# Attention and a routed expert layer on one core: one-hots shared 17, 9 and 6, the seatless test moved up, rank products and idle products around the last tile's rows

## What is computed

```python
x = x + xattn(layernorm(x), ctx, ctx)      # 8 heads of 8 rows, softmax over 256 columns
h = layernorm(x)
logits = h @ gate                          # 8 experts
w, idx = top_k(logits, 2); w = softmax(w)
for each token, for its two experts e:
    out += w[e] * (silu(h @ w0[e]) * (h @ w1[e])) @ wo[e]
x = x + out
```

## Time and profile before

| | |
|---|---|
| median of 3 runs | 489.21 us (484.64 to 489.81) |
| the profiled execution's own time | 489.81 us |
| its span (first to last instruction) | 488.1 us |
| mean granted TensorE clock | 0.931 |
| TensorE matmul busy | 426.1 us, 87% |
| VectorE busy | 303.1 us, 62% |
| ScalarE busy | 267.1 us, 55% |
| GpSimd busy | 219.9 us, 45% |

### The profile page before, as it was taken

How to read it: one execution, slowest core, us unless ns; L and a number is a source line. 1 busy time by engine, 2 the same in 40 slices (tenths; PEclk the granted TensorE clock), 3 DMA queues, 4 the chain that set the end, 5 groups by cost and what they waited for, 6 DMA issues and landing times.

```text
span 488.1 us, 10784 instructions
## 1 busy us (share of the span) xinstructions
PE 426.1 (87%) x3468; PEld 212.4 (44%) x3469; DVE 303.1 (62%) x636; ACT 267.1 (55%) x529; POOL 219.9 (45%) x244
## 2 busy tenths in 40 slices
PE   4857999889899999998666799999999999999991
PEld 4322343324343444333232455555555555566650
DVE  7799898898888888976867734343434343222220
ACT  2555898778778788977414444444444444222220
POOL 9544322181809052339628233454545454536231
PEclk9775899989889999999867999999999999999997
DMA  8757569685859682426994112333333333323322
GB/s 246 215 165 201 153 165 215 205 245 173 247 165 245 178 255 75 151 71 234 395 389 150 36 34 45 42 57 43 54 47 50 49 50 53 55 45 46 41 22 23
DMA packets 42246, 65.03 MB, mean 133 GB/s; under 512 B 6297, under 2 KB 32218, under 8 KB 42202
## 3 DMA queue, kind: packets, MB, share of 16 engines
q1 hardware_dynamic: 28570, 38.49, 28.0%
q0 software_dynamic: 11328, 23.86, 20.9%
q10 hardware_dynamic: 2304, 2.10, 1.4%
HBM read 39.53 MB, written 24.58 MB: 131 GB/s over the span
## 4 chain that ended last, share of the span: by engine, by line
PE 67%; DVE 10%; ACT 7%; DMA 6%; POOL 4%; issue 2%; ACTq 1%; SPq 1%; DVEq 0%; POOLq 0%
PE max_ps L1658 19%; PE pv_ps L1525 9%; PE pv_ps L1680 6%; PE ring_ps L1508 6%; ACT pt L851 5%; PE max_ps L1652 4%; PE max_ps L1384 4%; PE ring_ps L1680 4%; DVE mx L1026 4%; PE ring_ps L1616 3%; PE ring_ps L1405 2%; PE ring_ps L1675 2%; DMA Q<-mrow 2%; DMA Q<-q_img 2%; PE ring_ps L1416 2%
## 5 line engine op out<-in xcount | busy, mean ns | idle before, releaser
L1026 DVE TENSOR_REDUCE mx<-max_ps 128x4 f32<-128x1024 f32 x128 | 150.7, 1218 | 20.7 <-PE max_ps L1384 20.6
L851 ACT ACTIVATE pt<-ring_ps 128x512 f32<-128x512 f32 x256 | 139.2, 599 | 32.6 <-PE ring_ps L1508 29.1
L1658 PE MATMUL max_ps<-w_sb,pt 128*128 x224 | 101.6, 596 | 1.0 <-issue 1.0
L778 POOL DMA_INDIRECT out<-rb,sidx x34 | 54.8, 1613 | 81.3 <-DVE rb L1358 37.0
L1525 PE MATMUL pv_ps<-pt,w_sb 128*27 128x256 f32 (+2 forms) x1024 | 82.7, 408 | 0.7 <-ACT pvs L861 0.4
L1330 DVE TENSOR_TENSOR pt<-pt,max_ps 128x512 f32<-128x512 f32 x34 | 23.4, 688 | 68.4 <-issue 49.2
L1384 PE MATMUL max_ps<-K,Q 48*128 48x256 bf16 x512 | 54.5, 294 | 12.2 <-DVE mx L1026 12.0
L1508 PE MATMUL ring_ps<-Q,K 50*128 50x256 f16 x512 | 53.4, 289 | 11.5 <-ACT pt L851 9.2
L1658 PEld LDWEIGHTS max_ps<-w_sb,pt 128*128 128x128 f32 x224 | 40.3, 190 | 42.2 <-issue 42.0
L935 ACT ACTIVATE pt<-ring_ps 128x512 f32<-128x512 f32 x34 | 20.3, 598 | 68.1 <-PE ring_ps L1616 68.1
L1508 PEld LDWEIGHTS ring_ps<-Q,K 50*128 50x128 bf16 x512 | 15.1, 96 | 65.3 <-ACT pt L851 58.2
(11 more groups left out here) (230 smaller groups left out, 650.6 us busy)
## 6 DMA issues: line engine op xcount, KB each, us to landing
w_sb<-in_L_ffn_w_kernel POOLq DMA_DIRECT2D x16, 512.0 KB, 12.4
K<-k_img SPq DMA_DIRECT2D x14, 448.0 KB, 6.2
Q<-q_img SPq DMA_DIRECT2D x14, 448.0 KB, 7.6
k_img<-kpart SPq DMA_DIRECT2D x28, 192.0 KB, 3.8
q_img<-qpart SPq DMA_DIRECT2D x28, 192.0 KB, 3.4
wo_sb<-in_L_ffn_wo_kernel POOLq DMA_DIRECT2D x8, 512.0 KB, 14.4
acc<-pvs SPq DMA_DIRECT2D x6, 512.0 KB, 3.1
wo_sb<-in_ctx ACTq DMA_DIRECT2D x16, 128.0 KB, 3.9
```

The source lines that it names most:

```text
L778: g.indirect_dma_start(xacc, bass.IndirectOffsetOnAxis(ap=sidx[sl.par][:, 0:1], axis=0), y_sb[sl.par], None, compute_op=ALU.add).then_inc( ...
L851: a.activation(pt[:, (2 * i + h) % PTN, :, :], bank(key)[:, :, :], ACT.Exp, scale=SCALE).then_inc(ring_read, 1)
L1026: v.tensor_reduce(mx[:, t % 2, :, :, p].rearrange("q mt h -> q h mt"), max_ps[n % 2][:, :, :, :], axis=AX.X, op=ALU.max).then_inc(max_read, 1)
L1658: last = nc.tensor.matmul(flat(max_ps[sl.par][:, bank_of]), lhsT=xT[sl.par][:, k * P:(k + 1) * P], rhs=weight(w, e, KC, k), start=(k == 0) ...
```

## The change

It has four parts. In the last tile, the reordering of tile 14 moves from head 2 to head 1, the transposes and logits of units 5 and 6 move one head later, rank product 0 moves to head 6 and rank product 1 behind the last reordering and the logits of tile 14, followed by two new idle products into the bank of `pv_ps`; VectorE's rank sums move to match. The one-hots are shared 17 (VectorE), 9 (ScalarE) and 6 (GpSimd), where it was 16, 8 and 8. The first half of the seatless test moves in front of the first gathered rows on TensorE and in front of the weight products on VectorE, and its second half moves from slot 1 to slot 0.

```diff
-    rows_at[T - 1, 1] = ST - 3
-    logits_at[T - 1, 2] = ST - 3
-    rows_at[T - 1, 3] = ST - 2
-    logits_at[T - 1, 4] = ST - 2
-    unperm_at = {(T - 2, 1): 0, (T - 2, 4): 1, (T - 1, 2): 2}
+    rows_at[T - 1, 2] = ST - 3
+    logits_at[T - 1, 3] = ST - 3
+    rows_at[T - 1, 4] = ST - 2
+    logits_at[T - 1, 5] = ST - 2
+    unperm_at = {(T - 2, 1): 0, (T - 2, 4): 1, (T - 1, 1): 2}
...
-    ranks_at = {(T - 1, 2): 0, (T - 1, 7): 1}
+    ranks_at = {(T - 1, 6): 0}
...
-        by_act = [(k, t) for k in range(TOPK) for t in range(2, T, 4)]
-        by_pool = [(k, t) for k in range(TOPK) for t in range(3, T, 4)]
+        by_act = [(0, t) for t in (3, 7, 11, 14)] + [(1, t) for t in (2, 5, 8, 11, 14)]
+        by_pool = [(0, t) for t in (5, 10, 15)] + [(1, t) for t in (4, 9, 13)]
+        by_dve = [(k, t) for k in range(TOPK) for t in range(T) if (k, t) not in by_act + by_pool]
...
             norm_last(normed_last[0:2], x2_last[0:2], 0, 1)
-            ranks(0)
...
             norm_last(normed_last[2:3], x2_last[2:3], 2, 2)
-            ranks(1)
+            ranks(0)
...
             norm_last(normed_last[3:4], x2_last[3:4], 3, 3)
+            ranks(1)
             choose(ST, unit_tiles[ST])
...
             then(v.tensor_tensor(pay[:, 1], wts[:, :, :], pay[:, 0], ALU.subtract))
+            v.wait_ge(spare_turned, 1)
+            then(v.tensor_reduce(spare_any[:, :], y_ps[1][0:NT, 0, P // 2:P].bitcast(f16), axis=AX.X, op=ALU.max))
+            v.tensor_tensor(spare_diag[:, :], identh[0:NT, 0:NT], spare_any[:, 0:1].broadcast_to([NT, NT]),
+                            ALU.mult).then_inc(diag_done, 1)
             v.wait_ge(rows_picked, TOPK)
...
                 if sl.peeled and sl.t == 0:
-                    turned_spares()
+                    spread_back()
...
-            def keep_warm(n):
+            def keep_warm(n, to=max_ps[1][:, 1]):
 
                 for _ in range(n):
-                    nc.tensor.matmul(flat(max_ps[1][:, 1]), lhsT=ident[:, :], rhs=flat(xn), start=True, stop=True)
+                    nc.tensor.matmul(flat(to), lhsT=ident[:, :], rhs=flat(xn), start=True, stop=True)
...
             for m in range(ST - 1, UNITS):
                 turn_rows(m)
                 logits(m)
+                if m < UNITS - 1:
+                    rank(1)
+                    keep_warm(2, pv_ps)
...
             pe.wait_ge(slots_done, 1)
+            turn_spares()
             turn_x(Slots(0, 0))
...
                 if sl.peeled and sl.t == 0:
-                    turn_spares()
+                    spread_spares()
                 if sl.peeled and sl.t == 1:
-                    spread_spares()
                     slot_weights()
```

More of the change, by code:

```diff
@@ L1232, in _ @@
                                 iota_t[:, None, :].broadcast_to([P, T, NTL]), ALU.is_equal).then_inc(rows_picked, 1)
-                onehots(k, [t for t in range(T) if (k, t) not in by_act and (k, t) not in by_pool])
+                onehots(k, [t for n, t in by_dve if n == k])
             v.wait_ge(told_full, 1)
@@ L1302, in stage, with spread_back @@
                     v.tensor_copy(wo_st[n][:, 0:FC // 2, :], wo_sb[:, bass.ds(e * FC, FC // 2), :]).then_inc(wo_copied[0], 1)
-            def turned_spares():
-                v.wait_ge(spare_turned, 1)
-                then(v.tensor_reduce(spare_any[:, :], y_ps[1][0:NT, 0, P // 2:P].bitcast(f16), axis=AX.X, op=ALU.max))
-                v.tensor_tensor(spare_diag[:, :], identh[0:NT, 0:NT], spare_any[:, 0:1].broadcast_to([NT, NT]),
-                                ALU.mult).then_inc(diag_done, 1)
-                then(v.tensor_scalar(rtok[:, :], tok[:, :], 1.0, None, ALU.max))
-                then(v.reciprocal(rtok[:, :], rtok[:, :]))
-            def slot_rows():
+            def spread_back():
                 v.wait_ge(spare_full, 1)
@@ L1316, in slot_rows @@
                 v.wait_ge(spare_read, 1)
+                then(v.tensor_scalar(rtok[:, :], tok[:, :], 1.0, None, ALU.max))
+                then(v.reciprocal(rtok[:, :], rtok[:, :]))
+            def slot_rows():
                 then(v.tensor_tensor(spare_of[:, :], spare_of[:, :], spare_own[:, :], ALU.add))
@@ L1584, in _ @@
                     else:
-                        pe.wait_ge(told_done, k * T // 2 + t // 4 * 2 + t % 4 + 1)
+                        pe.wait_ge(told_done, by_dve.index((k, t)) + 1)
                     last = nc.tensor.matmul(pv_ps[:, 0, 0:NTL], lhsT=onehot_s[:, k, t, :], rhs=onehot_t[:, k, t, :],
```

## The result

The changed kernel takes 484.31 us in the median of 20 runs (478.84 to 489.14), the kernel before 488.60 in the median of 20 beside them (482.71 to 493.13). The ratio is 0.9927, 95% interval 0.9898 to 0.9956: 0.7% faster. That is 3.6 us by the ratio (as by the means of all 20) and 4.3 by the medians, where I forecast 4.2. Executions of either kernel scatter by 2.6 to 2.7 us (standard deviation), so whole times can't tell parts of 1 us; the rows can.

The account below looks back on a forecast made before the run. TensorE bounds the expert stage; before it a chain across engines, where only shortening the last-ending piece saves time. Terms 1.0 + 0.6 + 1.4 - 0.1 + 1.3 = 4.2 us off the 489.21 median give 485.0 us, range 482.8 to 488.8.

Parts of the forecast that it names:

- F: Stretch from GpSimd's first weight load to its first one-hot, forecast to shorten by 1.6 us.
- the slot weights: Slot 1: TensorE's 1.28 us wait for VectorE's reading of the spread spares goes; 1.3 us saved, bounds 0.9 and 1.4.
- The last tile's heads: TensorE, last tile: two waits removed, one added; last reordering starts 1.0 us sooner, bounds -0.5 and 1.8.
- Rival C: Clock falls to half in head 1 at the added wait, until the tile's end; 4.6 us slower, 493.8, chance 0.05.
- One of my signs of being wrong: Last tile: the last reordering starts no sooner after head 0 than before.
- VectorE's moved sums hidden: Last tile: moved rank sums fit VectorE's waits, 1 us to spare for the first, about 0.7 for the second; no loss.
- Idle products: Before the last rows: they keep TensorE's clock up for gate products and transposes; 0.6 us saved, bounds -0.9 and 0.7.
- full clock from 243 on: Sign of being right, last tile: TensorE's clock stays full from 243 on, with gate products at 0.58 us.
- One-hots: GpSimd's one-hots cut from eight to six, so the sum product ends earlier; 1.4 us saved, bounds 0.9 and 1.6.
- VectorE's 17 would not hold GpSimd up: One-hots: GpSimd runs beside VectorE and ends at 261.7; the rival that it is held up had chance 0.06.
- The seatless test: Its transposition moves before the first gathered transposes on TensorE; costs 0.1 us, bound -0.3; VectorE's added work hidden.
- The idle products behind the sum: After the one-hots' sum: six records take 4.5 to 5.4 us, up to 0.5 us late at half clock.

Follow-up runs that it names:

- e8: Kernel before with only the seatless test moved up; median 488.20 us against 489.22 beside it, ratio 0.9890.
- e3: Changed kernel without the two idle products behind the moved rank product; median 485.35 us, ratio to the kernel before 1.0025.
- e4: Changed kernel with two idle products instead of three behind the one-hots' sum; median 485.66 us, ratio to the kernel before 0.9965.
- e7: Kernel before with only the one-hots shared 17, 9 and 6; median 487.30 us against 489.22 beside it, ratio 0.9969.
- e6: Kernel before with only the part around the last tile; median 487.40 us against 489.22 beside it, ratio 0.9995.
- e11: Changed kernel, copy before head 1's exponentials, two and a half idle products behind the one-hots, half one behind the first transposes; 482.07 us, ratio 0.9913.
- e12: e11 plus an idle product behind the last slot's hidden layer and half a one behind its transposes; 481.93 us, ratio to the kernel before 0.9851.
- e2: Changed kernel with tile 14's reordering put back at head 2; median 483.36 us, ratio to the kernel before 0.9937.
- e1: Changed kernel with the whole part around the last tile undone; median 485.64 us, ratio to the kernel before 0.9992.

## Why the prediction was right, and where it was not

The time came out at 484.31 against 485.0, the gain at 3.6 (interval 2.1 to 5.0) or 4.3 by the medians, against 4.2. The mechanism was right in the back half and for the order of the heads at full clock; that the total came so near is in part luck. F gave half of its 1.6 us on average, the slot weights gave more than forecast, and the 489.21 from which I took the gain was 0.6 above the median of twenty. Point by point:

1. The last tile's heads, 1.0 us, set between 1.3 at full clock and 0.45 at half. At full clock the heads came as I had counted them (the last reordering 15.84 us after the first weight load, forecast 15.87), and against the old order that is 1.04, not 1.3. The step that failed is the clock. I let it act on the last two heads, and it fell in heads 1 and 2, behind the wait that the change adds; U was then 0.3 longer than before, in three of five traces. Rival C had this mechanism with the right place; it overpriced it, because the clock was back within 4 us each time. One of my signs of being wrong came true: from head 0's scores to the last reordering the changed kernel took 17.83 us, the kernel before 17.56. What I missed beside it: 0.64 us of wait at the rank product was not the wait's size but what the low clock left of it (1.39 in e8).
2. VectorE's moved sums hidden: right, 0.97 and 0.73 us to spare (forecast 1 and 0.7).
3. Idle products, 0.6 us: right. The gate products gained 0.41 in every trace. From the last reordering to the last choice, traces with an equally long last normalisation differ by 0.59 between the orders (8.09 and 7.50 us with 0.41, 8.37 and 7.78 with 0.69) and by 0.66 between e3 and the others. The idle products ended at 243.3, and the transposes of the last rows began at 244.75. The sign "full clock from 243 on" held up to 248.5 only; then it was half for 3.4 us, where before it was half from 242.9 to 253.1. One thing not foreseen: the last normalisation took 0.69 us instead of 0.41, and from the last reordering to the last choice the changed kernel needs 7.78 us where e4 needs 7.50; 0.3 us of F went there.
4. One-hots, 1.4 us: 1.45, in every trace that has them. That VectorE's 17 would not hold GpSimd up was read rightly from the trace (6.58 us for six, forecast 6.6). The Trainium skill, "SBUF — State Buffer", Who interferes with whom, says that tensor_scalar can enter two-port modes, in which one of the two engines blocks the other fully. No such block came here: GpSimd's one-hots took 0.84 to 0.97 us beside VectorE's and 0.79 with VectorE idle. Whether VectorE's ran in such a mode no trace shows.
5. The seatless test, -0.1: 0.06 to 0.2 (e4). The idle products behind the sum, "up to 0.5 us late": up to 0.85 (e8: X 6.88 against 6.03), because six records took 5.47 us at half clock throughout. My own numbers gave 0.8 and not 0.5 (262.0 + 5.4 = 267.4 against 266.6). It was outside my sum, and it should have been in it: in six of the seven traces that have the moved test and three idle products, X is 0.2 to 0.85 above 6.03 (mean of the seven 6.44, against 5.90 in the three traces without the moved test).
6. Slot weights, 1.3 us: 1.56 at the first output product. I had counted TensorE's idle of 1.28 and not the 0.3 us of the spreading product, which moved in front of slot 0's `turn_inter`, where TensorE waits anyway (0.47 us before, 0.51 after).

By stretches: F gives 0.75 us (mean of old order 33.12, of new with idle products 32.37; four traces each), S 1.45, O 1.54, and X takes 0.3 (the changed kernel's own 6.20 and 6.22) to 0.5: 3.2 to 3.4 us, inside what the whole time shows. That S and O come from the one-hots and the seatless test is shown by the runs that have one part alone (e7, e8) and by e6, which has neither.

## What to carry to other kernels

Take out a wait only after asking what the same engine stands for next at the other clock level: the wait in the trace (0.64 us) was 1.39 with the clock up, and the wait that replaced two others cost little itself but stood where the clock then fell. A stand behind another engine's queue can be cured by the order on that other engine: one copy put in front of two exponentials took 0.7 us off F at like clock (31.14 to 30.45; 1.0 off U, of which a slower normalisation took 0.3) and 2.3 against the traces where the clock had fallen. Idle products have two prices, their length at half clock and the gap that they leave; splitting them and putting the pieces into the gaps (e11, e12) met neither price, though with two traces that is a likely cure and not a proven one.

## What the runs showed of the hardware

- The granted clock falls in places that repeat: heads 5 to 7 in three of four traces of the old order, heads 1 and 2 in three of five of the new one, none in four with the copy first. In the new order the fall came at the end of the stand of 1.75 us, and in e2 at the second of two of 0.7; with the copy first the stand is 0.48. In the old order a stand of 0.94 to 0.97 us had ended 2 to 3 us before the fall, and e8, where it was 0.75, did not fall. What makes it fall is not shown.
- The last normalisation (256 columns, VectorE) took 0.69 or 0.70 us in ten of the fourteen traces, of both orders, and 0.41 in before, e1, e2 and e4. GpSimd had begun to issue a weight load 0.14 us earlier in all fourteen, so that alone is not the cause. It stays open.
- GpSimd's first weight load, in head 0 of the last tile, came between 216.6 and 224.2 us after the span's start, 7.6 us apart, in executions whose attention code up to there is the same. The rest of the span varied by 5.5 us over the same traces, changes included.
